# Two transformer layers in one kernel: weight pieces of the out-projection stage two steps ahead, biased sums one per step, bias rows padded to 128

## The reference, cut to what matters

```
# layer 0
x = x + out @ Wout
h2 = layer_norm(x, ln2_g, ln2_b)
x = x + (gelu(h2 @ W1 + b1) @ W2 + b2)
# layer 1
def act_quant(x):                       # per row
    s = 127.0 / clip(max(abs(x), -1), EPS)
    return clip(round(x * s), -128, 127) / s
def weight_quant(w):
    s = 1.0 / clip(mean(abs(w)), EPS)
    return clip(round(w * s), -1, 1) / s
def bitlinear(x, w, b):
    return act_quant(x) @ weight_quant(w).T + b
# adaln: rmsnorm(x, g) * (1 + scale) + shift, scale and shift from bitlinear(c, ...)
qkv = bitlinear(adaln(x, c, g1, w_ada1, b_ada1), w_qkv, b_qkv)
x = x + bitlinear(attention, w_proj, b_proj)
h = gelu(bitlinear(adaln(x, c, g2, w_ada2, b_ada2), w_fc1, b_fc1))
x = x + bitlinear(h, w_fc2, b_fc2)
```

## Time and profile before

| | |
|---|---|
| median of 3 runs | 4202.47 us (4201.59 to 4207.68) |
| profiled execution, its own time | 4206.6 us |
| its span in the profile | 4204.8 us |
| mean granted clock of TensorE | 0.957 |
| busy: PE, DVE, ACT, POOL | 92%, 66%, 64%, 21% of the span |
| stage C (1412 to 1717 us) | 305 us |
| stage M (1717 to 2515 us) | 798 us |
| stage D (2515 to 2705 us) | 190 us |
| stage F (3800 us to the end) | 405 us |

### The profile page before, as it was taken

One profiled execution on the slowest core, in us unless ns is written; L12 is line 12 of the kernel. 1 busy time (PEld: TensorE's weight loads), 2 busy tenths in 40 slices (PEclk: granted clock), 3 DMA queues, 4 the chain that ended last, 5 costly groups with the idle time before them and its releaser, 6 DMA issues. The chain is left out here.

```text
span 4204.8 us, 70173 instructions
## 1 busy us (share of the span) xinstructions
PE 3877.2 (92%) x26756; PEld 2571.4 (61%) x26756; DVE 2793.8 (66%) x5147; ACT 2670.9 (64%) x4699; POOL 899.6 (21%) x1188
## 2 busy tenths in 40 slices
PE   8998999999999755689999969799999999997999
PEld 7885666666666444577778854366666666663444
DVE  4327888888888565434431227688888888886887
ACT  2227888888888422222222217598888888885887
POOL 0005555555555222100000016400000000002221
PEclk9998999999999877899999989899999999997999
DMA  5445333323232355434431226732323323214221
GB/s 185 182 164 129 64 64 74 67 59 64 59 64 47 104 170 169 148 126 150 150 115 51 76 71 245 263 75 59 64 61 73 69 59 64 59 29 136 69 70 43
DMA packets 307495, 419.49 MB, mean 100 GB/s; under 512 B 89365, under 2 KB 165673, under 8 KB 307159
## 3 DMA queue, kind: packets, MB, share of 16 engines
q1 hardware_dynamic: 307162, 415.00, 35.4%
HBM read 257.31 MB, written 157.32 MB: 99 GB/s over the span
## 5 line engine op out<-in xcount | busy, mean ns | idle before, releaser
L555 ACT ACTIVATE Sn<-Sn,mn 128x1024 f32<-128x1024 f32 x1024 | 1174.8, 1147 | 30.4 <-DVE mn L583 18.7
L521 PEld LDWEIGHTS pt<-ident,Sn 128*128 128x128 f32 x8192 | 880.9, 141 | 420.9 <-issue 412.9
L521 PE MATMUL pt<-ident,Sn 128*128 128x128 f32 x8192 | 1123.6, 280 | 1.6 <-DVE PT L547 0.9
L545 ACT ACTIVATE PT<-pt 128x512 f32<-128x512 f32 x1280 | 737.2, 597 | 236.9 <-PE pt L521 236.8
L489 PE MATMUL sp<-KS,QS 97*128 97x512 f32 (+1 forms) x2048 | 733.8, 440 | 44.4 <-DMA KS<-s_khi 22.9
L583 DVE CUSTOM_DVE_ANT_0 Sn<-sp,biastile 128x1024 f32<-128x1024 f32 x512 | 624.5, 1220 | 145.1 <-PE sp L489 113.5
L585 DVE TENSOR_SCALAR_CACHE_REDUCE Sn<-sp 128x1024 f32<-128x1024 f32 x512 | 624.3, 1220 | 136.6 <-PE sp L489 136.4
L628 POOL TENSOR_SCALAR biastile<-dist,ascale 128x1024 f32<-128x1024 f32 x512 | 573.9, 1121 | 499.7 <-DVE mn L583 484.9
L510 PE MATMUL po<-PT,Vp 128*32 128x256 f32 x8192 | 651.5, 391 | 0.0
L547 DVE COPY PT<-pt 128x512 f32<-128x512 f32 x768 | 531.3, 692 | 118.5 <-PE pt L521 118.5
L1044 ACT ACTIVATE gf<-pf,b1T 128x512 f32<-128x512 f32 x128 | 88.1, 688 | 562.0 <-PE pf L989 535.9
(11 more groups left out here) (230 smaller groups left out, 4923.3 us busy)
## 6 DMA issues: line engine op xcount, KB each, us to landing
QS<-s_qhi SPq DMA_DIRECT2D x128, 256.0 KB, 5.1
KS<-s_khi SPq DMA_DIRECT2D x128, 256.0 KB, 7.1
KS<-s_klo SPq DMA_DIRECT2D x64, 256.0 KB, 6.1
QS<-s_qlo SPq DMA_DIRECT2D x64, 256.0 KB, 6.9
Vp<-s_v SPq DMA_DIRECT2D x64, 256.0 KB, 7.9
s_o<-og SPq DMA_DIRECT2D x32, 512.0 KB, 8.7
xA<-in_x SPq DMA_DIRECT2D x8, 1024.0 KB, 5.8
s_qhi<-qstage SPq DMA_DIRECT2D x32, 256.0 KB, 2.0
```

What stands on the lines that cost most here:

```text
L521: op = nc.tensor.transpose(ps[:, i, :], sn[:, (g * HALF + i) * P:(g * HALF + i + 1) * P], K.ident[:])
L545: nc.scalar.activation(dst, src, ACT.Copy).then_inc(*s_cp_act.up())
L555: nc.scalar.activation(sn[:], sn[:], ACT.Exp, scale=-1.0, bias=mn[n % 3][:, t:t + 1], accum_out=sums[n % 5][:, t:t + 1]).then_inc(*s_exp.up())
```

## The change

**C.** The loads are split (`load_o`, `load_x`) and reordered. `load_w(2)` is issued ahead of the loop, and step s issues piece 3 + s/2 first of all, one piece, which is two steps, ahead of its use. Then come the store of x1 (tile s - 4), the stores of h2 (s - 7), and the loads. The inverse root is wholly POOL's (five small operations instead of one), the rounded half of h2 is ACT's; DVE loses four small operations per tile. Lags grow: h2 leaves a tile seven steps behind its load (before: four). `xC` has 5 buffers, `statC` 8, `hClo` 2.

The diff, cut:

```diff
-        o_l, x_l = S.loads("oC", 3, [P, D]), S.loads("xC", 4, [P, D])
+        o_l, x_l = S.loads("oC", 3, [P, D]), S.loads("xC", 5, [P, D])
...
         def sync_program():
             load_w(0)
-            load_tile(0)
+            load_o(0)
             load_w(1)
+            load_o(1)
+            load_x(0)
+            load_x(1)
             for dst, src in ((g2, a["L0_cond_ln2_g_cols"]), (b2, a["L0_cond_ln2_b_cols"]), (b2b, a["L0_cond_b2"].partition_broadcast(P))):
                 nc.sync.dma_start(dst[:], src).then_inc(*s_vec.up(16))
-            load_tile(1)
-            for s in range(NT + 4):
-                if s + 2 < NT:
-                    load_tile(s + 2)
-                if 0 <= s - 2 < NT:
-                    i = s - 2
+            load_o(2)
+            load_w(2)
+            for s in range(NT + TAIL):
+                if s % 2 == 0 and 3 + s // 2 < len(pieces_w):
+                    load_w(3 + s // 2)
+                if 0 <= s - 4 < NT:
+                    i = s - 4
                     sp.wait_ge(s_xb, i + 1)
                     buf, sem = xb.of(i)
...
-                if s % 2 == 0 and 2 + s // 2 < len(pieces_w):
-                    load_w(2 + s // 2)
-                if 0 <= s - 4 < NT:
-                    i = s - 4
+                if 0 <= s - 7 < NT:
+                    i = s - 7
                     rows = slice(i * P, (i + 1) * P)
                     sp.wait_ge(s_lo, i + 1)
...
+                if s + 3 < NT:
+                    load_o(s + 3)
+                if s + 2 < NT:
+                    load_x(s + 2)
...
         def tensor_program():
-            for s in range(NT + 4):
+            for s in range(NT + TAIL):
+                if 0 <= s - 2 < NT:
+                    project(s - 2)
+                if 0 <= s - 5 < NT:
+                    turn_h(s - 5)
                 if s < NT:
...
+        def h_high(i):
+            buf = hi.room(act, i)
+            act.wait_ge(s_hT, i + 1)
+            nc.scalar.activation(buf[:], hT[i % 2][:], ACT.Copy).then_inc(*s_hi.up())
...
+            for s in range(NT + TAIL):
                 if 0 <= s - 2 < NT:
                     i = s - 2
...
+                    dve.wait_ge(s_x, i + 1)
+                    nc.vector.bn_stats(st[i % 8][:, 0:6], x_l.at[i][0][:]).then_inc(*s_bn.up())
+                if s < NT:
+                    o_low(s)
+                if 0 <= s - 2 < NT:
+                    i = s - 2
+                    dve.wait_ge(s_bn, i + 1)
+                    nc.vector.bn_aggr(st[i % 8][:, 6:8], st[i % 8][:, 0:6]).then_inc(*s_ag.up())
                 if s % 2 == 0 and 2 + s // 2 < len(pieces_w):
                     split_lo(2 + s // 2)
...
+                if 0 <= s - 6 < NT:
+                    h_low(s - 6)
                 if 0 <= s - 1 < NT:
...
+                    residual(s - 1)
+                if 0 <= s - 3 < NT:
+                    normalise(s - 3)
...
+        def inverse_root(i):
+            t = st[i % 8]
+            v, r, w = t[:, 8:9], t[:, 9:10], t[:, 10:11]
+            pool.wait_ge(s_ag, i + 1)
...
+            pool.wait_ge(s_vec, 48)
+            for i in range(NT):
+                inverse_root(i)
+                buf = xb.room(pool, i)
+                nc.gpsimd.tensor_tensor(buf[:], x_l.at[i][0][:], b2b[:], ALU.add).then_inc(*s_xb.up())
...
                 if f == 0 and i > 0:
                     store_x2(i - 1)
+                if i > 0 and 0 <= f - 2 < TPB:
+                    store_x2b(i - 1, f - 2)
                 if u + 1 < len(work):
                     sync_work(*work[u + 1])
                 if 1 <= u <= len(work):
                     sync_store(*work[u - 1])
-                if f == 4:
+                if f == 4 and i + 1 < NBLK:
+                    load_h2(i + 1)
+                if f == 8:
                     for t in range(TPB):
-                        rows = slice(i * BLK + t * P, i * BLK + (t + 1) * P)
+                        rows = rows_of(i, t)
                         x, s = x_l.take(sp, (i, t), 1, (s_xst, 16 * (TPB * i + t + 1)), (s_xb, TPB * i + t + 1))
                         nc.sync.dma_start(x[:], K.x1_s[rows, :]).then_inc(*s.up(16))
-                    if i + 1 < NBLK:
-                        load_h2(i + 1)
             store_x2(NBLK - 1)
+            for t in range(TPB):
+                store_x2b(NBLK - 1, t)
...
-                    dve.wait_ge(s_bpb, 16)
-                    for t in range(TPB):
-                        k = TPB * i + t
-                        dve.wait_ge(s_x2, k + 1)
-                        if k:
-                            dve.wait_ge(s_xbst, 16 * k)
-                        nc.vector.tensor_tensor(xb2[:], x_l.at[i, t][0][:], bpb[:], ALU.add).then_inc(*s_xb.up())
+                if u >= FC + 2 and 0 <= u % FC - 2 < TPB:
+                    with_bias(u // FC - 1, u % FC - 2)
                 if u < len(work):
                     vector_work(*work[u])
+            for t in range(TPB):
+                with_bias(NBLK - 1, t)
         sync_program()
...
+    rows, rest = S.sb("brow" + name, [P, n], BF16), S.sb("brest" + name, [6, n])
...
     def split():
+        nc.vector.memset(rows[:], 0.0).then_inc(*dve.own.up())
+        dve.settle()
         dve.wait_ge(s_raw, 16)
-        nc.vector.tensor_copy(rows[:], rest[:]).then_inc(*dve.own.up())
+        nc.vector.tensor_copy(rows[0:6, :], rest[:]).then_inc(*dve.own.up())
         dve.settle()
-        nc.vector.tensor_tensor(rest[:], rest[:], rows[:], ALU.subtract).then_inc(*dve.own.up())
+        nc.vector.tensor_tensor(rest[:], rest[:], rows[0:6, :], ALU.subtract).then_inc(*dve.own.up())
         dve.settle()
...
-        xT = [S.sb(f"xTD{i}", [P, DC, P], BF16) for i in range(2)]
-        rc, rT = [S.sb(f"rcD{i}", [P, 6], BF16) for i in range(2)], [S.sb(f"rTD{i}", [6, P], BF16) for i in range(2)]
+        xT = [S.sb(f"xTD{i}", [P, DC + 1, P], BF16) for i in range(2)]
+        rc = [S.sb(f"rcD{i}", [P, P], BF16) for i in range(2)]
...
-            nc.tensor.matmul(pr[w][:], rT[i % 2][:], brow[:, cols], start=False, stop=True).then_inc(*s_m[w].up())
+            nc.tensor.matmul(pr[w][:], xT[i % 2][:, DC, :], brow[:, cols], start=False, stop=True).then_inc(*s_m[w].up())
...
-            nc.scalar.activation(rT[i % 2][:], px[0:6, D:D + P], ACT.Copy)
-            nc.scalar.activation(xT[i % 2][:], px[:, 0:D].rearrange("p (c q) -> p c q", q=P), ACT.Copy).then_inc(*s_xT.up())
+            nc.scalar.activation(xT[i % 2][:], px[:, 0:D + P].rearrange("p (c q) -> p c q", q=P), ACT.Copy).then_inc(*s_xT.up())
...
             load_tile(1)
-            nc.sync.dma_start(braw[:], a["L1_cond_b_fc1"].partition_broadcast(3)).then_inc(*s_b1.up(16))
+            load_bias(a["L1_cond_b_fc1"])
             nc.sync.dma_start(w1[:], K.tern_s["fc1"].rearrange("(c p) n -> p c n", p=P)).then_inc(*s_w1.up(16))
             load_tile(2)
             nc.sync.dma_start(bf2[:], a["L1_cond_b_fc2"].partition_broadcast(P)).then_inc(*s_bf2.up(16))
-            sp.wait_ge(s_blow, 1)
-            nc.sync.dma_start(brow[1:2, :].bitcast(F32), blow[1:2, :].bitcast(F32)).then_inc(*s_row.up(16))
+            place_bias()
             nc.sync.dma_start(w2[:], K.tern_s["fc2"].rearrange("(c p) n -> p c n", p=P)).then_inc(*s_w2.up(16))
             for b in range(1, B):
                 load_b(b)
             for s in range(NT + TAIL):
...
         def gpsimd_program():
...
+            for buf in rc:
+                nc.gpsimd.memset(buf[:], 0.0).then_inc(*pool.own.up())
+            pool.settle()
+            pool.wait_ge(s_winv, 1)
+            for s in range(NT + TAIL):
+                if 0 <= s - 4 < NT:
+                    i = s - 4
+                    pool.wait_ge(s_sx, i + 1)
+                    scale(i, 9, 7, 2).then_inc(*s_dqx.up())
+                    if i >= 2:
+                        pool.wait_ge(s_Tx, i - 1)
+                    inverse_pieces(K, rc[i % 2], col(i, 10), col(i, 8), winv[:], s_rc)
+                    pool.wait_ge(s_bf2, 16)
+                    buf = xo.room(pool, i)
+                    pool.wait_ge(s_xq, i + 1)
+                    nc.gpsimd.tensor_tensor(buf[:], x3[i % 4][:], bf2[:], ALU.add).then_inc(*s_xb.up())
+                if 0 <= s - 3 < NT:
+                    if (s - 3) % LT == 0:
+                        ready_b((s - 3) // LT, s_G)
+                    inverse_root(s - 3)
+                if s < NT:
+                    pool.wait_ge(s_so, s + 1)
+                    scale(s, 2, 0, 1).then_inc(*s_dqo.up())
+                if 0 <= s - 5 < NT:
+                    i = s - 5
```

More of the change, by code:

```diff
@@ L695, in stage_outproj @@
         xh = [S.sb(f"xhC{i}", [P, D]) for i in range(2)]
-        st = [S.sb(f"statC{i}", [P, 12]) for i in range(4)]
+        st = [S.sb(f"statC{i}", [P, 12]) for i in range(8)]
         hT = [S.sb(f"hTC{i}", [P, DC, P]) for i in range(2)]
-        hi, lo = S.stores("hChi", 3, [P, DC, P], F32R), S.stores("hClo", 3, [P, DC, P], F32R)
```

(53 more changed lines are left out.)

309 lines of the change are left out of this document (119 added, 190 removed).

## The result

The changed kernel takes **4011.05 us** (median of 4 runs, 4010.46 to 4014.39) against 4202.74 us before (4 runs, 4201.59 to 4207.68): ratio 0.9543, 95% interval 0.9527 to 0.956.

A forecast was written before the change was run, and what follows sets the result against it. No engine was full in C, where PE waited for late weight pieces; D and F were near PE's bound. C -88, M -20, D -16, F -23 sum to -147, giving 4055.5 us; range about 4020 to 4115, without POOL's rival.

The forecast's parts named there:

- C, the period of 6.0 us: Stage C: pieces loaded ahead cut the period per tile from 8.85 to 6.0 us, -88 us (ends -107 and -60).
- DMA 0.56 x 305/32 = 5.3: Stage C: DMA work of 5.3 us per tile, taken as the nearest bound after the change.
- small waits: Stage C: small waits of one engine for another remain above DMA's 5.3 us, so 6.0 was taken.
- M, -20: Stage M: earlier loads at block boundaries, -4.9, -13.1 and -6, against +4 at the end; ends -10 and -27.
- D, -16: Stage D: 128-row bias matmuls remove a 0.19 us gap per group, period 5.25 to 4.7; ends -20 and 0.
- F, -23: Stage F: thirty tiles at -1.2 give -36, later head +14, end -1; ends -40 and -8.
- C at the low clock: Rival, stage C: PE stays at 1.2 GHz, 6.9 us a tile, C gives -60, time 4083; 16%.
- C at the DMA bound, 5.4 a tile: Rival, stage C: DMA binds at 5.4 us a tile, C gives -107, time 4037; 18%.
- the zero rows buy nothing: Rival, D and F: padding the bias matmul leaves the gap, D gives 0, time 4094; 13%.
- F's head not late: Rival, stage F: tile 3's load lands in time, F gives -40, time 4038; 8%.
- POOL's stretching: Rival, stage F: POOL's small operations take 1.84 us each, F +467, time 4520; 3%.
- The high end of the forecast's span: About 4115 us: C at the low clock, D's rows worth nothing, M at -10.

The follow-up runs named there:

- the run with more traffic: Changed kernel with one more 128x384 load (197 KB) in every second step of C, into a buffer nobody reads: 4010.0 us.
- once the buffers no longer bind: Kernel of 3986.2 us (changed kernel with heads, M's end and loads reordered) with hClo at three buffers, xC five, statC two: 3977.4 us.
- with six rows: Changed kernel with bias matmuls over 6 rows instead of 128, in D and F: 4056.9 us.
- 64 rows: Changed kernel with bias matmuls over 64 rows instead of 128, in D and F: 4047.5 us.

## Why the prediction was wrong, point by point

**C, the period of 6.0 us: this step failed**, and with it the number. The mechanism was right: ACT's waits for the pieces went, and the clock with them came back. The size was wrong: the period was 4.49, not 6.0. "DMA 0.56 x 305/32 = 5.3" divides all DMA work of the stage by 32 tiles, but the 31 intervals it was held against leave out the head (Wout, the first tiles) and the tail, where part of that work lies. And I read a share of busy DMA time as work that adds up to a floor: the run with more traffic carries 338 GB/s at the same period, so the changed kernel's 320 would fit into some 4.25 us a tile (an estimate, 4.49 x 320/338). Then I put 0.7 us on top for "small waits" with no row behind it. What bound C in place of the DMA engines, the round trip of the two `hClo` buffers, stands nowhere in the forecast. Measured: 31 x (4.49 - 8.85) = -135, and +3.6 outside the intervals: the first sum comes 1.7 us sooner (14.3 for 16.1 us after the stage's first issue), and the drain is 5.3 us longer (18.2 for 12.8), as h2 leaves three steps later. That drain I had put at 0. DVE's work, put at 4.2 to 4.6 a tile, measured 4.0 (127.83/32): the row to trust, as DVE is the fullest engine once the buffers no longer bind, at 4.12.

**M, -20:** -20.6. The first boundary gave 4.7 (forecast 4.9), the next three 19.4 (19.1), the end cost 4.2 (4); the other intervals gave 0.7 together. The load stands 7.8 us behind the first store, not 6.9. That the sum met the number to 0.6 us is in part luck: other kernels with the same M lie up to 3.6 us longer.

**D, -16:** -13.3. The group went to 1.08 as forecast. In 22 of 31 intervals between starts of `pqD` the period is 4.49 (2456.80 to 2461.29), below the 4.7 of the sum; with six rows it is 5.11, so the padding gives 0.62 of it. The other nine take 5.0 to 7.0 us, most of them at the sequence boundaries, where PE waits for `xqD` (4.4 us in 3 waits behind 2400) and DVE for the adaLN row (9.1 in 3); before, four were longer than 5.3. From first to last the mean went from 5.44 to 4.98. The head costs 0.9. "172 of 190 us busy" was read from a window that leaves out D's head and tail: in D's true bounds PE is busy 172 of 214.9 us at a mean granted clock of 0.90, and DVE 147.9.

**F, -23:** -29.0. Tile 1's fc1 is 15.0 us later, counted from the stage's start (forecast +14); thirty tiles give -42.8, 9.91 a tile (forecast -36, 10.13); the tail -1.2 (-1). The steady period fell by 1.30, from 11.33 to 10.03, and not by 1.2; and the interval from tile 1 to tile 2 fell by 5.0, from 12.85 to 7.89, so that part of what the late head costs is won back at once.

**The rivals.** C at the low clock fell: the granted clock is 1.00 in the middle of C, although PE waits there for `xhC` alone 20 times, 13.9 us in all. The Trainium skill, page "TensorE: Matmul & The Clock Gate", section "A second HAM failure mode: psum-queue depth-cycling", would have the clock swing with such pauses; this trace doesn't agree. C at the DMA bound, 5.4 a tile, fell as well: it was the low end of my range, and as a floor the cause of the miss. That the zero rows buy nothing fell by the run with six. The rule of the Trainium skill, page "TensorE: Matmul & The Clock Gate", section "Why this matters for your kernels", that a matmul with K = 32 takes the time of one with K = 128, agrees with the matmul itself here (0.39 us with 6 or 64 rows, 0.38 with 128); the 0.2 us lie beside it. F's head not late fell; the first fc1 came 18.0 us later, where 3846 against 3828.64 had meant 17.4. POOL's stretching fell: in F POOL is busy 185 of 373 us, with the means of its small operations at 0.19 to 0.56 us. The high end of the forecast's span, put at about 4115, adds up to 4109.5 (4055.5 + 28 + 16 + 10).
